# Summing sixteen expert outputs: the first halving addition shared between VectorE and GpSimd

## The reference, cut to what matters

```python
logits = einsum('bsh,eh->bse', tokens, gate_w)            # 16 experts
weights = softmax(logits, axis=-1)
top2_w, top2_idx = top_k(weights, 2)
y = relu(einsum('nh,edh->ned', flat, expert_w) + expert_b)
sel = take_along_axis(y, flat_idx[:, :, None], axis=1)
out = sum(sel * flat_w[:, :, None], axis=1)               # sum over experts
...
x = x + gb * out                                          # flat = layernorm(x) * (1 + cb) + sb
```

## Time and profile before

| what | value |
|---|---|
| median of 3 runs | 1212.86 us (1210.7 to 1214.95) |
| the profiled execution | 1215.1 us |
| its span in the trace | 1213.3 us |
| expert part, first to last modulation on GpSimd | 1084.76 to 1210.33 us |
| VectorE busy, 1131.8 to 1148.1 us | 15.72 of 16.30 us |
| TensorE busy, the same stretch | 16.09 of 16.30 us |
| ScalarE, GpSimd busy, the same stretch | 14.48 and 3.64 us |
| TensorE clock granted there | 1.00 |

### The profile page before, as it was taken

One profiled execution on the slowest core, in us unless ns is written; L12 is line 12 of the kernel. 1 busy time (PEld: TensorE's weight loads), 2 busy tenths in 40 slices (PEclk: granted clock), 3 DMA queues, 4 the chain that ended last, 5 costly groups with the idle time before them and its releaser, 6 DMA issues. The chain is left out here.

```text
span 1213.3 us, 33822 instructions
## 1 busy us (share of the span) xinstructions
PE 1068.4 (88%) x11683; PEld 733.6 (60%) x11683; DVE 879.7 (73%) x2948; ACT 818.5 (67%) x2658; POOL 661.1 (54%) x1070
## 2 busy tenths in 40 slices
PE   6699994799999998798899999997996778799996
PEld 4467673377777776465577777775663577654442
DVE  4799997588888886374788888885547312079998
ACT  3688883588888887323888988884327403178886
POOL 1578995788888886111888888882106300002222
PEclk9899997799999998989999999998997899899998
DMA  7000000112222121311112111111001486600000
GB/s 232 2 2 11 11 2 1 27 45 55 57 52 54 45 46 45 117 32 34 41 44 47 45 44 45 45 45 27 1 1 44 92 194 137 142 5 16 16 18 18
DMA packets 69566, 58.79 MB, mean 48 GB/s; under 512 B 42262, under 2 KB 53442, under 8 KB 69122
## 3 DMA queue, kind: packets, MB, share of 16 engines
q1 hardware_dynamic: 69411, 56.83, 19.3%
HBM read 29.40 MB, written 2.38 MB: 26 GB/s over the span
## 5 line engine op out<-in xcount | busy, mean ns | idle before, releaser
L1168 PE MATMUL psum<-wa_wqkv,wa_hT 128*128 128x512 f32 x384 | 189.8, 603 | 4.4 <-DVE wa_tmp L1032 3.2
L1124 ACT ACTIVATE wa_p<-psum,wa_nb 128x128 f32<-128x128 f32 x512 | 183.7, 398 | 4.3 <-DVE wa_nb L1048 4.2
L1048 DVE CUSTOM_DVE_ANT_0 psum<-psum,wa_bias 128x128 f32<-128x128 f32 x512 | 133.0, 323 | 51.2 <-PE psum L1197 51.2
L1014 POOL TENSOR_TENSOR wa_p<-wa_p,wa_rrs 128x512 f32<-128x512 f32 x128 | 133.2, 1040 | 47.7 <-DVE wa_rrs L1057 47.7
L1594 POOL TENSOR_TENSOR ex_total<-ex_total,mod 128x128 f32<-128x128 f32 x32 | 15.5, 485 | 218.3 <-DVE ex_total L1722 218.3
L1124 ACT ACTIVATION_READ_ACCUMULATOR wa_p<-psum,wa_nb 128x1 f32 x512 | 122.2, 239 | 0.0
L1840 PE MATMUL psum<-ex_wc,ex_hT 128*128 128x512 f32 x256 | 117.6, 602 | 3.4 <-DVE ex_yw L1705 2.2
L1769 ACT ACTIVATE ex_yw<-psum,ex_w 128x128 f32<-128x128 f32 x384 | 106.7, 400 | 20.1 <-DVE ex_w L1698 7.4
L985 POOL TENSOR_TENSOR wa_qr<-wa_qr,wa_tmp 128x512 f32<-128x512 f32 x64 | 81.8, 1278 | 64.3 <-DVE wa_tmp L1032 64.3
L1134 ACT ACTIVATE wa_pT<-psum 128x512 f32<-128x512 f32 x128 | 76.6, 598 | 39.7 <-PE psum L1177 39.7
L1381 ACT ACTIVATE ml_gelu<-psum,ml_b 128x512 f32<-128x512 f32 (+1 forms) x48 | 32.9, 685 | 85.0 <-PE psum L1408 71.6
(11 more groups left out here) (256 smaller groups left out, 2978.2 us busy)
## 6 DMA issues: line engine op xcount, KB each, us to landing
wa_vm<-wa_v SPq DMA_DIRECT2D x127, 128.0 KB, 2.3
cv_toep<-cv_zpad SPq DMA_DIRECT2D x32, 256.0 KB, 4.5
cv_toep<-cv_zpad SPq DMA_DIRECT2D x16, 512.0 KB, 6.9
wa_tabs<-in_rotations_dram SPq DMA_DIRECT2D x2, 2048.0 KB, 8.2
wa_rows<-y_rows SPq DMA_DIRECT2D x31, 128.0 KB
wa_rows<-y_rows SPq DMA_DIRECT2D x31, 127.0 KB
x_rows<-in_L_attn_x_dram SPq DMA_DIRECT2D x4, 512.0 KB, 6.0
out_dram<-x_rows SPq DMA_DIRECT2D x32, 64.0 KB, 1.5
```

The source lines that it names most:

```text
L1014: nc.gpsimd.tensor_tensor(p, p, cols_bc(rrs[:, t % 2, r, :], P), ALU.mult)\
L1048: m = nc.vector.tensor_tensor_reduce(out=s, in0=s, in1=edges, scale=-1.0, scalar=MAX_FLOAT, op0=ALU.add, op1=ALU.min, accum_out=nb[:, t % ...
L1124: e = nc.scalar.activation(pr[:, t % 2, r, h, :], sim_bank[r][:, P * h:P * h + P], ACT.Exp, bias=nb[:, t % 2, r, h:h + 1], scale=-1.0, acc ...
L1168: nc.tensor.matmul(bank, hT[:, t % 3, :], wqkv[:, INNER * k:INNER * k + INNER], start=True, stop=True).then_inc(done.sem, 1)
```

## The change

The sum of 16 becomes two independent sums of 8 that are done at the same time. VectorE's `halve(0)` adds bank 1 to bank 0 (512 numbers instead of 1024) and so waits for ScalarE's first ReLU group instead of its last. A new stage `upper_half` on GpSimd adds bank 3 to bank 2, in place, after ScalarE's second and third groups. `halve(1)` then adds the two results, and waits for GpSimd as well. `halve(2)` and `halve(3)` are as before.

```diff
-    v_half = in_turn("v_half", 4)
+    v_half, g_half = in_turn("v_half", 4), signal("g_half")
...
-            return Phase([(residual, UP_LAG + 2)], 0, TILES)
+            def upper_half(t):
+                for k in (2, 3):
+                    relu_done[k].wait(gp, t)
+                y = yw[:, t % 2]
+                a, b = NE // 2, 3 * NE // 4
+                nc.gpsimd.tensor_tensor(y[:, a:b, :], y[:, a:b, :], y[:, b:NE, :], ALU.add).then_inc(g_half.sem, 1)
+
+            return Phase([(upper_half, UP_LAG), (residual, UP_LAG + 2)], 0, TILES)
...
-                    n = NE >> (k + 1)
+                    n = max(NE >> (k + 1), 1) if k else NE // 4
...
                         relu_done[0].wait(dve, t)
-                        relu_done[3].wait(dve, t)
+                        relu_done[1].wait(dve, t)
                     else:
                         v_half[k - 1].wait(dve, t)
+                    if k == 1:
+                        g_half.wait(dve, t)
...
-                    nc.vector.tensor_tensor(to, y[:, 0:n, :], y[:, n:2 * n, :], ALU.add).then_inc(v_half[k].sem, 1)
+                    other = y[:, NE // 2:NE // 2 + n, :] if k == 1 else y[:, n:2 * n, :]
+                    nc.vector.tensor_tensor(to, y[:, 0:n, :], other, ALU.add).then_inc(v_half[k].sem, 1)
```

## The result

Before 1213.26 us (median of 4 runs), the changed kernel 1224.91 us (1222.79 to 1229.38, 4 runs). The ratio is 1.0087, 95% interval 1.0054 to 1.012. The forecast was 1206.8, and the change moved the other way.

What follows compares the result with a forecast made beforehand. VectorE was taken as the bound, then TensorE at 15.5 us a group. Gains of 2.5, 2.4, 0.9, 0.9 and 0.4 less 1.0 at the end gave 6.1 us: 1206.8 from 1212.86, range 1203 to 1216.5.

Steps and rivals of the forecast that it cites:

- What bounds: Expert part: VectorE never stops in a plain tile, 3.66 us; a group of four tiles takes 16.29.
- TensorE's need of at most 15.5 and 3.46: TensorE needs at most 15.5 us of a group's 16.29 and 3.46 of a plain tile's 3.66.
- The conflict and the size of a turn: VectorE and GpSimd block each other on SBUF reads; GpSimd's addition end to VectorE's fourth addition end (H): 2.35 us.
- The new chain: ScalarE, GpSimd's addition, then turns with VectorE: two steps take 7.34 us with normalization, 7.00 without; one step 3.67 or 3.50.
- Gating: VectorE's gating operations, 1.65 us a group: 1.27 stays in the chain, giving 15.3; TensorE's 15.5 is taken.
- The two-step chain also halves what a single slow step costs: The chain of fourth-addition ends spans two steps, so a group takes (4 x 7.34 + 1.27) / 2 = 15.3 us.
- The end: From H(30), the end of tile 30's fourth addition, to the last residual addition's end: 3.98 us before, 5.0 after.
- The rivals: TensorE bounds after all, 1213.9 or 1211 (0.24); longer turns, 1219 (0.18); no conflict on reads, 1203.5 (0.08).
- The slower one: Blocked operations take full duration, 3.06 us instead of 2.35 to H: some 6 us slower, 1219; chance 0.18.
- If it starts ahead of GpSimd's: Sign of error: VectorE's half of the first addition starts before GpSimd's, so GpSimd is late and the wait long.

Runs made afterwards that it cites:

- the third buffer: Kernel before, undivided, with three buffers instead of two for the 16 outputs: 1211.14 us, ratio 0.9962; timed again 1207.88 us, ratio 0.9948.
- the further wait: Changed kernel, with GpSimd's addition of tile t also waiting for VectorE's fourth addition of tile t-1: 1216.71 us, ratio 1.0015 against the kernel before.
- The even form: Changed kernel with the further wait, where plain steps are even at 3.77 us: 1216.71 us, ratio 1.0015 against the kernel before.

## Why the prediction was wrong, point by point

- **What bounds.** VectorE is the bound: right, though 0.28 of its 3.66 in a plain step was a wait for its own result and a turn lost to GpSimd, as the third buffer showed. TensorE's need of at most 15.5 and 3.46 was too high; with GpSimd's reads gone a group took 14.82 and plain steps 3.27. Taking 15.5 for a group rested on that, and was right by no measurement.
- **The conflict and the size of a turn.** Right for the additions, and the most exact part: 2.34 measured in the run with the further wait, for 2.35. That the conversion, with one input, would be held as well was not foreseen. GpSimd's addition: 1.27 forecast, 1.274 measured.
- **The new chain.** This is the step that failed. It let VectorE's fourth addition of tile t-1 go ahead of GpSimd's addition of tile t in the order of turns, and took all steps as equal. By its own numbers, in a plain step of 3.50, VectorE's fourth addition asks 3.21 us after H(t-1) and GpSimd's next addition after 3.38 (0.09 + 3.20 + 0.09): a lead of 0.17, which I did not see as a condition. With one long step the next GpSimd addition comes first; the fourth addition then waits 1.24, ScalarE idles, does two tiles in a row, and that puts the following GpSimd addition first again. In a group the steps are not equal: before, they ranged from 3.66 to 4.42, by more than the lead. The further wait, which keeps that order, took away some 7.4 of the 9.9 us of the part, although it also starts GpSimd's addition later; filling instead of reading took away 20.2; an addition of 0.73 instead of 1.27 took away 5.3.
- **Gating.** "The two-step chain also halves what a single slow step costs": not borne out, nor tested. The even form is no two-step chain, for the further wait ties each step to the one before; there a group takes 16.58 for a forecast of 15.5, and the kernel is 0.15% slower than before, not 0.5% faster. What the order would give without that wait, no run shows.
- **The end.** Forecast 1.0 us longer. In the changed kernel it was 0.14 shorter, since GpSimd's last new addition was done before H(30), inside the collision. In the even form, with the further wait, it was 5.05 for the forecast 5.0 (H(30) at 1210.25, last residual addition's end at 1215.30); that is luck in part, since the new addition ended 1.72 after H(30) and not 1.12, and VectorE's half ran ahead of it, unblocked.
- **The rivals.** The slower one had the right sign and about half the size (6 us for 11.7), but by another mechanism: the turns have the length that I gave them, there is one more of them in each pair of plain steps, and it is the longest. "If it starts ahead of GpSimd's" stood among the signs of being wrong; the mirror image, GpSimd's ahead of VectorE's last, did not.
- **The range.** 1203 to 1216.5 left 1224.9 out; it was built from errors in durations, and the error was in an order.

## What to carry to other kernels

Where two engines share something for the length of an instruction, write down for every short operation on the critical path which long one of the other engine may start just ahead of it, and by how much it leads; here a lead of 0.17 us was lost as soon as one step was longer. Moving work to an idle engine paid here only in the run where that work didn't read what the busy one reads; where it does, a wait that keeps the order can be worth more than the overlap. Before sharing work, look whether a third buffer frees the engine that is the bound: here it gave 5.7 us of the part where the division lost 9.9.

## What the runs showed that was not expected

- A GpSimd addition of 1.29 us held up a VectorE conversion of 128x8, an operation with one input, for 1.26 us (0.15 alone). A GpSimd fill of the same length left the additions beside it alone but held the same conversion just so, for 1.24 and 1.16 us, the two times that they met.
- A steady pattern need not be the even one: the same instructions gave steps of 5.09 and 2.89 us without the further wait and 3.77 with it.
- A ReLU that waits for its own engine's addition two tiles back starts 0.18 us later for it, although that addition is just ahead of it in order; without that wait a step was 0.28 shorter, 0.10 of it because the two engines' order of reading turned round as well.
